# Attention stage: the probabilities of a head are scaled before the square and low part of the shared FFN are made

## What is computed

```python
xn = layernorm(x)
# attention: 16 heads of 32 channels, one shared key and value head
q, k, v = xn @ w_q.T, *split(xn @ w_kv.T)
q, k = rotary(q), rotary(k)
attn = softmax(where(causal, -max, q @ k.T))
attn_out = (attn @ v) @ w_proj.T + b_proj
# shared part of the FFN, with 1024 inner channels
shared = square(relu(xn @ shared_up_w.T)) @ shared_down_w.T
# routed part: 8 of 32 experts for each token
routed = experts(xn @ fc1_w.T, chosen by gate_w) @ fc2_w.T
out = x + attn_out + shared + routed
```

## Time and profile before

| | us |
|---|---|
| median of 3 runs | 2185.95 (2183.76 to 2187.13) |
| the profiled execution | 2200.01, its span 2198.5 |
| stretch of `middle` in the trace | about 200 to 1385 |
| stretch of `experts` and `combine` | about 1385 to 2198 |

### The profile page before, as it was taken

How to read it: one execution, slowest core, us unless ns; L and a number is a source line. 1 busy time by engine, 2 the same in 40 slices (tenths; PEclk the granted TensorE clock), 3 DMA queues, 4 the chain that set the end, 5 groups by cost and what they waited for, 6 DMA issues and landing times. The chain is left out here.

```text
span 2198.5 us, 43820 instructions
## 1 busy us (share of the span) xinstructions
PE 1814.4 (83%) x10080; PEld 1350.6 (61%) x10081; DVE 1169.2 (53%) x3293; ACT 885.5 (40%) x2473; POOL 819.6 (37%) x704
## 2 busy tenths in 40 slices
PE   5604878888888888887888888679999999999969
PEld 5603665666656656566566566457777777777744
DVE  7696665756647656556476565223333333333325
ACT  3311553544636636445366355123333233333311
POOL 0041331322323323223223132246666666666630
PEclk9956999999999999999999999899999999999989
DMA  8863332332333333323232342797777677777769
GB/s 300 310 249 59 106 99 80 112 92 88 103 93 103 100 89 107 98 86 108 90 89 93 94 120 74 231 245 115 117 116 113 110 118 117 117 116 116 116 157 360
DMA packets 191390, 286.23 MB, mean 130 GB/s; under 512 B 30582, under 2 KB 133118, under 8 KB 188002
## 3 DMA queue, kind: packets, MB, share of 16 engines
q0 software_dynamic: 60528, 96.90, 23.2%
q1 hardware_dynamic: 75602, 121.45, 17.8%
q10 hardware_dynamic: 55104, 66.19, 10.2%
HBM read 128.07 MB, written 134.14 MB: 119 GB/s over the span
## 5 line engine op out<-in xcount | busy, mean ns | idle before, releaser
L1240 POOL DMA_INDIRECT sums<-e_y,e_row x288 | 447.2, 1553 | 312.9 <-DVE e_y L1228 147.2
L720 POOL DMA_INDIRECT slot_rows<-m_row,m_idx x256 | 261.6, 1022 | 756.9 <-ACT m_sc L772 666.3
L772 ACT ACTIVATE m_sc<-m_sc,m_low 128x512 f32<-128x512 f32 (+3 forms) x512 | 282.7, 553 | 381.3 <-DVE m_low L896 340.6
L1269 PE MATMUL e_psH<-e_w,e_xt 128*128 x1152 | 323.3, 403 | 0.2
L896 DVE CUSTOM_DVE_ANT_0 m_sc<-m_psS,cst 128x512 f32<-128x512 f32 (+3 forms) x512 | 239.9, 488 | 124.9 <-PE m_psS L1039 79.5
L1269 PE MATMUL e_psY<-e_w,e_ht 128*128 x1152 | 299.7, 383 | 0.0
L1228 DVE TENSOR_SCALAR e_y<-e_psY,e_row 128x256 f32<-128x256 f32 x288 | 139.4, 484 | 241.1 <-DMA sums<-e_y,e_row 127.4
L1039 PE MATMUL m_psS<-m_ks,m_qs 96*128 96x256 f32 (+2 forms) x512 | 181.8, 397 | 77.0 <-DVE m_low L896 68.9
L1221 DVE TENSOR_SCALAR e_relu<-e_psH 128x256 f32<-128x256 f32 x288 | 122.3, 425 | 225.1 <-PE e_psH L1269 206.8
L1203 ACT ACTIVATE e_xt<-e_psX 128x256 f32<-128x256 f32 x288 | 110.4, 383 | 276.1 <-PE e_psX L1258 172.0
L1269 PEld LDWEIGHTS e_psH<-e_w,e_xt 128*128 128x128 f32 x1152 | 196.5, 190 | 40.8 <-issue 3.4
(11 more groups left out here) (178 smaller groups left out, 3133.1 us busy)
## 6 DMA issues: line engine op xcount, KB each, us to landing
e_row<-slot_rows ACTq DMA_DIRECT2D x288, 144.5 KB
m_qs<-m_qhi SPq DMA_DIRECT2D x264, 64.0 KB, 2.0
e_w<-in_w SPq DMA_DIRECT2D x64, 256.0 KB
m_qs<-m_qlo SPq DMA_DIRECT2D x132, 64.0 KB, 1.9
f_xt<-in_x SPq DMA_DIRECT2D x8, 1024.0 KB, 9.0
xnt_hi<-f_hi SPq DMA_DIRECT2D x8, 1024.0 KB, 4.2
xnt_lo<-f_lo SPq DMA_DIRECT2D x8, 1024.0 KB, 7.4
sums<-empty POOLq DMA_DIRECT2D x32, 256.0 KB, 2.9
```

The source lines that it names most:

```text
L720: pool.indirect_dma_start(out=xs, out_offset=bass.IndirectOffsetOnAxis(ap=idx[u][:, k:k + 1], axis=0), in_=row[u][:, :], in_offset=None).t ...
L772: nc.scalar.activation(cols, cols, ACT.Exp, bias=low[:, h % 2, i:i + 1], scale=-1.0, accum_out=total[:, h % 2, i:i + 1]).then_inc(exp_done, 1)
L1240: pool.indirect_dma_start(out=sums[u % 2], out_offset=bass.IndirectOffsetOnAxis(ap=row[u % NR][:, ROW - 1:ROW].bitcast(U32), axis=0), in_= ...
L1269: mm = pe.matmul(out[u % 2][:, 0:INTER], lhs[u % 2][:, c * P:(c + 1) * P], w[:, bass.ds(e * W + c * INTER, INTER)], start=(c == 0), stop=( ...
```

## The change

In `middle`, in the slot loop of DVE, the call of `scale(s)` now stands ahead of the call of `shared(s)`. Nothing else is changed: the same instructions, the same waits, the same order on PE, ACT, POOL and SP.

```diff
                     if s - 2 in Q_AT:
                         rotate(b, f"q{Q_AT[s - 2]}", (1,))
                     if s < NH:
+                        scale(s)
+                    if s < NH:
                         shared(s)
-                    if s < NH:
-                        scale(s)
                     if s - 2 in Q_AT:
                         low_part(b, f"q{Q_AT[s - 2]}")
```

## The result

| | before, us | changed, us | ratio (95% interval) |
|---|---|---|---|
| medians, first comparison | 2186.5 | 2246.8 (2238.7 to 2252.3) | 1.027 (1.023 to 1.030) |
| the same kernels again, later, where the kernel before takes longer | 2203.1 | 2250.8 (2249.2 to 2255.2) | 1.023 (1.020 to 1.026) |
| profiled executions, span | 2198.5 | 2250.7 | |

The changed kernel is slower by 48 to 60 us. The forecast was 2216, with a range up to 2245: the sign and the slower ring were right, the size was half, and what is missing in it is mainly TensorE's clock.

The account below looks back on a forecast made before the run. The prediction took a ring through DVE and ACT to bound `middle`, with PE beside it in slack. Changes by kind of slot summed to 3.78 us a turn, +30.2 us over 8 turns: 2186.0 becomes 2216.2, range 2200 to 2245.

Parts of the forecast that it names:

- the slower ring: In `middle`, `down`, scores of block 256, mask, exponentials, scaling, square, low part: 6.90 us a plain slot against 6.56; chance 0.68.
- TensorE's clock: Rival in `middle`: clock falls in PE's 1.99 us wait for `down`, in 32 of 96 slots; 39 us more, 2255; chance 0.13.

## What to carry to other kernels

Moving a step ahead of another on one engine fills a wait there, but ask who waits for the step that now comes last, and what stands in line behind that waiter: here `down`, and behind it the scores that feed the same step. A wait of TensorE that is off the critical path is not free once it gets as long as those behind which the trace already shows the clock falling. Where such a wait can't be closed, repeated matmuls in it can pay (2247 to 2224, and 1.006 to 0.997).

## What the runs showed of the hardware

- The scaling takes longer where a scatter of GpSimd starts just ahead of it. In slot 7 of turn 1 POOL started 0.03 ahead of the scaling, which took 1.54 and not 1.27; the multiplication of 384 columns alone took 0.69 and not 0.41. It happened in 12 of the 128 slots, 0.28 each, always with a scatter of line 702 that had started 0.025 to 0.029 us before; ten more that had started 0.002 to 0.023 before cost nothing. In slot 14 of before the two overlapped at no cost. That the scatter is the cause is read from this coincidence; no run parts the two. The rule of the Trainium skill (SBUF — State Buffer, Who interferes with whom), that of a `tensor_scalar` in a two-port mode and a GpSimd instruction the later one waits in full, fits neither: the scatter ran for 0.99.

```profile
260.50 1.54 DVE L906 TENSOR_SCALAR m_sc<-m_sc,m_inv 128x128 f32<-128x128 f32 x4
```

```profile
260.47 0.99 POOL L702 DMA_INDIRECT slot_rows<-empty,m_pidx  x1 [0.30 <-issue]
```

- Falls of the clock are not a property of one wait. Of 83 waits of 1.9 to 2.4 us in the inner slots of the changed kernel 18 were followed by one. In turns 1 to 4 that was the wait at the end of slot 11 and no other inside (it was 2.30 and not 2.03 there, since a scatter held up the scaling; waits as long in slots 1, 7 and 9 had no fall), in turns 5 to 8 it was in other slots too. Why these, no run here tells. Over the 13 traces of this case, the longer the wait of PE in an inner slot (0 and 15 left out), the more often the clock fell in it or in the 3 us behind it:

| wait of PE, us | waits | with a fall |
|---|---|---|
| 0.9 to 1.3 | 465 | 0 |
| 1.3 to 1.7 | 180 | 10 |
| 1.7 to 1.9 | 30 | 4 |
| 1.9 to 2.1 | 144 | 24 |
| 2.1 to 2.5 | 176 | 76 |
| 2.7 to 3.1 | 59 | 40 |
| over 3.2 | 4 | 4 |
